# Writing and reading back the third attention's turned weights in two halves

## The reference, cut to what matters

```python
q = (xq @ Wq + bq).reshape(B, L, 16, 16)              # 4 x 1024 rows, 16 heads of 16
k, v = ...                                            # 77 keys, from the context
scores = einsum('bqhd,bkhd->bhqk', q, k) / sqrt(16)
attn = softmax(scores, axis=-1)                       # the weights: 16 x 77 per row
out = einsum('bhqk,bkhd->bqhd', attn, v).reshape(B, L, 256)
return x_q + (out @ Wp + bp)
```

## Time and profile before

| | us |
|---|---|
| median of 3 runs (lowest, highest) | 991.32 (990.92, 993.13) |
| the profiled execution's own time | 993.48 |
| its span, from the first to the last instruction | 991.7 |
| TensorE busy | 931.4 (94%) |
| VectorE busy | 869.5 (88%) |
| ScalarE, GpSimd busy | 743.9 (75%), 701.0 (71%) |
| DMA packets of 16 engines | 205354 |

### The profile page before, as it was taken

How to read it: one execution, slowest core, us unless ns; L and a number is a source line. 1 busy time by engine, 2 the same in 40 slices (tenths; PEclk the granted TensorE clock), 3 DMA queues, 4 the chain that set the end, 5 groups by cost and what they waited for, 6 DMA issues and landing times. The chain is left out here.

```text
span 991.7 us, 32386 instructions
## 1 busy us (share of the span) xinstructions
PE 931.4 (94%) x10500; PEld 812.2 (82%) x10500; DVE 869.5 (88%) x4318; ACT 743.9 (75%) x1604; POOL 701.0 (71%) x1099
## 2 busy tenths in 40 slices
PE   6987899999999999999999999999999999998996
PEld 3775788888889898888888888888888888787884
DVE  2469999999999999999999999999999999887643
ACT  2345788888878888888878787888887887787763
POOL 1227867877777788787777777788777777666752
PEclk9679999999999999999999999999999999999999
DMA  8277200033333332223333332222333332210000
GB/s 285 61 145 136 65 18 18 15 75 74 72 71 76 77 75 51 61 56 75 76 69 72 76 76 51 63 62 67 76 72 70 76 77 52 60 37 7 6 7 18
DMA packets 205354, 66.43 MB, mean 67 GB/s; under 512 B 186520, under 2 KB 198961, under 8 KB 204546
## 3 DMA queue, kind: packets, MB, share of 16 engines
q1 hardware_dynamic: 205186, 64.35, 29.4%
HBM read 39.02 MB, written 25.30 MB: 65 GB/s over the span
## 5 line engine op out<-in xcount | busy, mean ns | idle before, releaser
L2333 PE MATMUL ps<-hT_C,w_m_sb 128*128 128x128 f32 x2048 | 256.6, 278 | 1.8 <-DVE hidden_C L1663 1.5
L2333 PEld LDWEIGHTS ps<-hT_C,w_m_sb 128*128 128x128 f32 x2048 | 243.6, 192 | 14.4 <-issue 8.2
L1032 ACT ACTIVATE silu_C<-ps,cols_sb 128x128 f32<-128x128 f32 x256 | 93.5, 366 | 120.0 <-PE ps L2333 115.5
L2344 PE MATMUL ps<-w_m_sb,hidden_C 128*128 128x256 f32 x512 | 121.1, 380 | 0.2
L1569 DVE MATCH_REPLACE8 scores_left_B<-mx_B,scores_left_B 128x77 f32<-128x77 f32 x512 | 108.4, 225 | 0.0
L1565 DVE MATCH_REPLACE8 scores_left_B<-mx_B,scores_B 128x77 f32<-128x77 f32 x512 | 108.1, 223 | 0.0
L2344 PEld LDWEIGHTS ps<-w_m_sb,hidden_C 128*128 128x128 f32 x512 | 92.7, 190 | 10.9 <-DVE hidden_C L1663 0.7
L650 POOL TENSOR_TENSOR p_B<-scores_B,mx_B 128x616 f32<-128x616 f32 x64 | 78.4, 1226 | 26.3 <-DVE mx_B L1563 24.9
L655 POOL TENSOR_TENSOR scores_D<-scores_D,mx_D 128x616 f32<-128x616 f32 x62 | 76.0, 1225 | 25.1 <-DVE mx_D L1636 25.1
L1663 DVE SCALAR_TENSOR_TENSOR hidden_C<-ps,cols_sb,silu_C 128x128 f32<-128x128 f32 x256 | 83.7, 337 | 9.7 <-ACT silu_C L1032 9.5
L1517 DVE TENSOR_REDUCE mx_A<-ps 128x8 f32<-128x1024 f32 x64 | 75.3, 1219 | 11.8 <-PE ps L2235 11.2
(11 more groups left out here) (188 smaller groups left out, 2451.7 us busy)
## 6 DMA issues: line engine op xcount, KB each, us to landing
p_turned_D<-p_blocks_D SPq DMA_DIRECT2D x100, 160.0 KB, 3.9
pT_D<-p_turned_D SPq DMA_DIRECT2D x25, 640.0 KB, 4.0
xn_turned_A<-xn_blocks_A SPq DMA_DIRECT2D x124, 32.0 KB, 2.0
xn_A<-xn_turned_A SPq DMA_DIRECT2D x31, 128.0 KB, 2.1
x_A<-in_x SPq DMA_DIRECT2D x28, 128.0 KB, 3.3
out<-y_D SPq DMA_DIRECT2D x28, 128.0 KB, 2.5
w_m_sb<-in_w_m SPq DMA_DIRECT2D x3, 1024.0 KB, 5.2
w_mod_sb<-in_w_mod SPq DMA_DIRECT2D x2, 1024.0 KB, 9.5
```

What stands on the lines that cost most here:

```text
L1032: sc.activation(SA[:, j, :], bank(f"C.up{j}")[:, 0:P], ACT.Silu, bias=col("bm1_a", j)).then_inc(sa_ok, 1)
L2333: ins = mm(bank(f"C.up{j}")[:, half * P:(half + 1) * P], w_m1[:, k, m:m + P], HT["C"][:, t % HT_COPIES["C"], k, :], start=(k == 0), stop=( ...
L2344: ins = mm(bank("C.dn0")[:, 0:CH], G[:, t % G_COPIES, j, :], w_m2[:, j, :], start=(j == 0), stop=(j == HJ - 1))
```

## The change

The DRAM tensor gets the half as its first dimension. `write_weights` and `read_weights` are called once per half: the write of a half waits for that half's turned blocks alone, and there are eight DMAs of half the size for four, and two reads for one. Each half has its own semaphores. `weigh_values` waits for half 0 before its first eight matmuls and for half 1 before the other eight. From the second such tile on, a write also waits for the read of the tile before. One load (`w_qd`) shares a semaphore with `w_q`, for which the first queries of B and D now both wait.

```diff
-        weights_turned = {s: nc.dram_tensor(f"p_turned_{s}", [ROWS, QUAD, NCH, ROWS, QUAD], F32, kind="Internal").ap()
+        weights_turned = {s: nc.dram_tensor(f"p_turned_{s}", [KC, ROWS, QUAD, HCH, ROWS, QUAD], F32, kind="Internal").ap()
...
-            def write_weights(t, s):
+            def write_weights(t, s, c):
                 if not weights_by_transfer(t, s):
                     return
-                sp.wait_ge(pb_ok[s], KC * (weight_transfers(t, s) + 1))
+                n = weight_transfers(t, s)
+                sp.wait_ge(pb_ok[s], KC * n + c + 1)
+                if n > 0:
+                    sp.wait_ge(pt_in[s][c], 16 * n)
                 for i in range(ROWS):
-                    sp.dma_start(weights_turned[s][:, :, :, i, :].rearrange("j k n q -> k n j q"),
-                                 PB[s][quad(i), :].rearrange("k (n j q) -> k n j q", n=NCH, j=ROWS)).then_inc(pb_out[s], 16)
-
-            def read_weights(t, s):
+                    sp.dma_start(weights_turned[s][c, :, :, :, i, :].rearrange("j k n q -> k n j q"),
+                                 PB[s][quad(i), c * HALF_COLS:(c + 1) * HALF_COLS].rearrange("k (n j q) -> k n j q", n=HCH, j=ROWS)
+                                 ).then_inc(pb_out[s][c], 16)
+
+            def read_weights(t, s, c):
...
-                sp.wait_ge(pb_out[s], 16 * ROWS * (weight_transfers(t, s) + 1))
+                sp.wait_ge(pb_out[s][c], 16 * ROWS * (weight_transfers(t, s) + 1))
                 sp.wait_ge(pv_ps[s], t)
-                sp.dma_start(PT[s][:].rearrange("p n q -> p (n q)"),
-                             weights_turned[s].rearrange("j k n i q -> (j k) (n i q)")).then_inc(pt_in[s], 16)
+                sp.dma_start(PT[s][:, c * HCH:(c + 1) * HCH, :].rearrange("p n q -> p (n q)"),
+                             weights_turned[s][c].rearrange("j k n i q -> (j k) (n i q)")).then_inc(pt_in[s][c], 16)
...
-                run(write_weights, i, 8, "D")
+                run(write_weights, i, 8, "D", 0)
+                run(write_weights, i, 8, "D", 1)
                 run(load_next_x, i, 0)
                 run(store_y, i, 9)
-                run(read_weights, i, 8, "D")
+                run(read_weights, i, 8, "D", 0)
+                run(read_weights, i, 8, "D", 1)
...
-            load_weights(w_qd[:], a["Wq"], "d")
+            load_weights(w_qd[:], a["Wq"], "b")
...
-                    dve.wait_ge(pb_out[s], 16 * ROWS * n)
+                    dve.wait_ge(pb_out[s][c], 16 * ROWS * n)
...
-                    pe.wait_ge(ld[{"A": "qkv", "B": "b", "D": "d"}[s]], 16)
+                    pe.wait_ge(ld["qkv" if s == "A" else "b"], 16 if s == "A" else 16 * 2)
...
             def weigh_values(t, s):
-                if weights_by_transfer(t, s):
-                    pe.wait_ge(pt_in[s], 16 * (weight_transfers(t, s) + 1))
-                else:
+                if not weights_by_transfer(t, s):
                     pe.wait_ge(pt_ok[s], 3 * weights_transposed(t, s) + 3)
...
                 for c in range(KC):
+                    if weights_by_transfer(t, s):
+                        pe.wait_ge(pt_in[s][c], 16 * (weight_transfers(t, s) + 1))
```

More of the change, by code:

```diff
@@ L214, in block_kernel @@
         ld = {n: sem(f"ld_{n}") for n in ("cond", "small", "mod_a", "mod", "gate", "rows", "qkv", "so",
-                                          "b", "kv_b", "kv_d", "up", "down", "d", "ctx")}
+                                          "b", "kv_b", "kv_d", "up", "down", "ctx")}
         silu_done, zeroed, masks_ok, rows_ok = (sem(n) for n in (
@@ L250, in block_kernel @@
         xb_ok, xb_out, xt_in = ({s: sem(f"{n}_{s}") for s in TURNED} for n in ("xb_ok", "xb_out", "xt_in"))
-        pb_ok, pb_out, pt_in = ({s: sem(f"{n}_{s}") for s in WEIGHTS_TURNED} for n in ("pb_ok", "pb_out", "pt_in"))
+        pb_ok = {s: sem(f"pb_ok_{s}") for s in WEIGHTS_TURNED}
+        pb_out, pt_in = ({s: numbered(f"{n}_{s}", KC) for s in WEIGHTS_TURNED} for n in ("pb_out", "pt_in"))
         tmp_ok, yd_ok, y_out = sem("tmp_ok"), sem("yd_ok"), sem("y_out")
@@ L487, in drain @@
                 store_y(TILES - 9)
-                write_weights(TILES - 8, "D")
-                read_weights(TILES - 8, "D")
+                write_weights(TILES - 8, "D", 0)
+                write_weights(TILES - 8, "D", 1)
+                read_weights(TILES - 8, "D", 0)
+                read_weights(TILES - 8, "D", 1)
                 write_turned(TILES - 1, "A")
@@ L492, in drain @@
                 store_y(TILES - 8)
-                write_weights(TILES - 7, "D")
-                read_weights(TILES - 7, "D")
+                write_weights(TILES - 7, "D", 0)
+                write_weights(TILES - 7, "D", 1)
+                read_weights(TILES - 7, "D", 0)
+                read_weights(TILES - 7, "D", 1)
                 store_y(TILES - 7)
```

## The result

The changed kernel takes 980.88 us (median; 980.28 to 984.83), the kernel before 992.23 (990.92 to 993.17; these are the three executions known before and one more). The ratio is 0.9897, 95% interval 0.9872 to 0.9922: 10.2 us, with 7.7 to 12.7 inside the interval. The forecast was 984.6 us, with a range from 982.5 to 989.5. The way came as forecast, and so did the wait that goes; the size was half as large again. Two executions further down, one of E2 (2691 us) and one of E4 (1840 us), were disturbed, and the medians and ratios leave them out.

What follows compares the result with a forecast made beforehand. VectorE was taken to bound every round, losing only TensorE's lateness beyond some 0.4 us. Listed waits of 6.6 us plus 0.3 made 6.9 us gone, taking 991.3 to 984.4, stated as 984.6 us, range 982.5 to 989.5.

Steps and rivals of the forecast that it cites:

- the wait that goes: VectorE's wait for `scores_a` ahead of `mx_A` would fall from 6.6 us to under 1; likeliest rival, chance 0.72.
- The chain: Late read of turned weights delays TensorE's `weigh_values`, which delays VectorE's `mx_A` by whatever exceeds some 0.4 us.
- The earlier start: Writes of half 0 start on SP after the first half's turn, 1.3 us before the second turn ends.
- the issues: Eight half-size writes on SP at 0.63 us each take 5.0 us, ending 3.7 us after the second turn.
- the queue of SP: After writes, x and y, SP is free and issues read 0 5.7 us after the second turn, read 1 at 6.0.
- The rule of the Trainium skill: Spoke against the change: small DMAs cost about 2 us fixed, and two transfers to disjoint halves serialize.
- The fit weighed there: DMA time as 2.0 us plus bytes at 436 GB/s: two serial reads of 320 KB would take 5.5 us.
- the sum: VectorE's 6.6 us of listed waits plus 0.3 us gives 6.9 us gone, median from 991.3 to 984.4.
- small gaps that would stay: Some 2.7 us of the 8.7 lost over 22 rounds, in scattered gaps on VectorE the change doesn't touch.
- The wait in the middle: TensorE's wait for half 1 inside `weigh_values`: cost bounded from nothing to 3.9 us, taken as nothing.
- my slack of 1.3 us for half 1: Half 1 would land 9.7 us after the second turn, 1.3 us before `weigh_values` needs it.

Runs made afterwards that it cites:

- E2: The changed kernel, unchanged, run again in more rounds: 980.90 us, ratio 0.9884 against the kernel before.
- E4: The kernel before with its four whole writes, but two reads by halves and two waits of TensorE: 986.91 us, ratio 0.9934.
- E1: The kernel before, unchanged, against itself: 990.88 us, ratio 0.9985.
- E12: The kernel before, unchanged, profiled a third time: one run, 995.98 us.
- E3: The changed kernel with its early half-size writes, but one read for both halves and one wait of TensorE: 985.49 us, ratio 0.9917.
- E11: Same kernel as E4 (the kernel before with two reads and two waits), run again for an undisturbed profile: 985.34 us, ratio 0.9934.
- E5: The changed kernel, but both halves' writes wait for both turns, so no earlier start: 998.64 us, ratio 1.0055 against the kernel before.
- E8: The changed kernel with the four writes of half 1 cut into eight, twelve writes in all: 1034.54 us, ratio 1.0415 against the kernel before.
- E7: The changed kernel with the load of `w_qd` on its own semaphore again: 981.57 us, ratio 0.9893 against the kernel before.
- E6: The changed kernel, but TensorE waits for both halves before its first matmul of `weigh_values`: 984.40 us, ratio 0.9912 against the kernel before.
- E10: The kernel before with its one read ahead of the load of x and the store of y: 991.24 us, ratio 1.0013.
- E9: The changed kernel with both reads ahead of the load of x and the store of y: 981.09 us, ratio 0.9903 against the kernel before.

## Why the prediction was off

*The chain* was right but for half of its last link. VectorE loses what TensorE is late beyond 0.4 us, and TensorE is late by the read. But the read is late in two ways, and I saw one: it is issued late because the writes land late (T0 + 7.7 in the round of the earlier trace rows), or it is issued in time and lands late itself. One of the worst rounds of before is of the second kind (timeline of all engines, 748 to 765 us; T0 is 749.24):

```profile
748.41 0.83 DVE L1509 STREAM_TRANSPOSE p_blocks_D<-p_D 128x640 f32<-128x640 f32 x1
...
756.16 0.32 SPq L410 DMA_DIRECT2D pT_D<-p_turned_D  x1
...
761.44 1.08 PE L2311 MATMUL ps<-pT_D,vblk_D 128*32 128x128 f32 x32 [1.67 <-DMA pT_D<-p_turned_D]
```

The read goes at T0 + 6.9, which by the prediction costs next to nothing, and TensorE starts 5.3 us behind it, not 4.0. Rounds whose read goes before T0 + 7.0 hold 4.0 of the 8.4 us of lateness in this profile, 7.4 of 11.7 in E1 and 5.8 of 10.0 in E12: more than half in all. That fits E3, where an earlier read alone doesn't cure it, and E11, where waiting part by part helps though the reads go as late as before. With the wait gone `mx_A` starts 13.05 to 13.11 us after T0 in 22 of 23 rounds, and at 13.42 in the other.

*The earlier start, the issues, the queue of SP* came nearly as worked out: T0 - 1.28 for - 1.3, 0.65 us an issue for 0.63, the eight done at T0 + 4.1 for 3.7, read 0 at T0 + 5.4 to 6.6, 6.1 at the median, for 5.7. The rule of the Trainium skill weighed there ("DMA: Bandwidth & Descriptors", "Rules for kernel authors") says that two transfers to disjoint partition halves serialize and aren't worth it. It did not decide here, where each half is half the columns of all 128 partitions: E11 gains some 6 us by two reads for one alone. E5 and E8 show where more and smaller transfers lose, in the time to issue: without the lead eight issues are a loss, and four more than the changed kernel's eight cost over 50 us (1034.5 against 981). The fit weighed there is, in the Trainium skill ("DMA: Bandwidth & Descriptors", "Anatomy of one DMA"), one of DMAs that GpSimd issues; by it a read of 320 KB would take 2.8 us, an estimate. SP issues the reads here, and in the changed kernel one of 320 KB landed 3.5 us after its issue at the median, which decides.

*The step that failed is the sum*: "What counts is VectorE's part: 6.6 us listed, plus [...] 0.3 us. 6.9 us are gone." That term was too small twice over.

- The list of waits under-reads. In the same profile the lateness by T0 is 8.4 us. The list leaves out small waits and shows the others some 0.1 short. The spacing of the rounds had said 8.7 plus the 0.8 of the first round; I put 2.7 of it down to small gaps that would stay (by the rows it is 2.9: 8.7 less the 6.6 listed, of which 0.77 belong to the first round and not to the spacing). Some 1.1 us stayed: the changed kernel has three rounds of 27.60 us, in places where before has long rounds too.
- One execution isn't the kernel. Three profiles of before have 8.4, 11.7 and 10.0 us, mean 10.0; three with the changed path (first profile, E2, E7) 0.4, 1.5 and 0.6, mean 0.8. The difference is 9.2 us, against 10.2, 11.5 and 10.6 by the ratios of the three. The profile I worked from has the lowest lateness of the three of before. But all three are of executions above the median (993.5, 996.4 and 996.0 us against 990.8 to 993.3 in the sets), so their mean may be on the high side.

*The wait in the middle* had the wrong sign. I looked for what it costs (0 to 3.9 us). E6 shows that it brings some 2 to 3: a read lands 4.0 us behind its issue at the median but up to 5.8 (before; a half 3.5 and up to 5.4, changed), and my slack of 1.3 us for half 1 was worked out from the median. What two parts and two waits give is room for late landings.

*How the parts share the gain,* by one profile each. Lead alone: lateness 3.9 (E3). Two reads alone: 4.8 (E11). Both with one wait: 4.4 (E6). All three: 0.8. From 10.0, each part takes most of the loss by itself and they overlap; halves without the lead make it 13.3, since they are paid in issues on SP.

*Open.* The ratios lie 1.0 to 2.3 us above the difference in lateness. All three profiles of before and E10 start late (first `mx_A` at 28.8 to 28.9 us), while of nine profiles with split reads or writes seven start at 26.2 to 27.0. The start counts in full: each of the thirteen profiled executions' own time, less its lateness and its first `mx_A`, is 953.6 to 957.2 us. The six that start late are all 1.2 us or more above the median of their kernel, up to 5.5; of the seven others six are within 1.6 of theirs (E6 is 2.2 above). From 12 to 30 us the granted clock is 0.85 or 0.86 in the six and 0.88 to 1.00 in the seven. That fits a start that is drawn anew in each execution and goes with the clock there; but no experiment touched the start, and whether the change makes the late one rarer isn't known. Nor is it known what makes single landings late. In the round of E8 shown above `mx_A` stands 3.62 us after TensorE's start, where 2.22 and the 0.86 of the stretched step make 3.08; the other 0.5 us wasn't looked into.

## What to carry to other kernels

Measure a loss by the distance between two events of a round that is fixed when nothing is late, over all rounds, and in more than one profile: a list of waits shows less, and a DMA's lateness differs from one execution to the next. Where a transfer lies on the path, plan for the worst landing, not the median; splitting it and waiting part by part buys room for it even where the bytes are the same. Every further DMA costs its issue on the queue that everything else stands in, so split only where something pays for that: two reads for one won 0.7% by themselves, eight writes for four on top made it 1% with a lead of 1.3 us, and without the lead a loss of 0.5%.

## What I had not expected of the hardware

An issue of a DMA with a four-dimensional pattern takes 0.57 us at best and 0.61 to 0.65 at the median, whether it moves 32 or 80 KB, or 40 and 80 mixed (E8); at 160 KB it is 0.57 and 0.90. Leaving x and y out from behind the writes (E10) doesn't let the writes land sooner. The kernel before scattered from 986.65 to 999.42 us over 23 runs on one chip, the changed path from 978.45 to 983.51 over 6 beside it (E9). The landings that vary may be the cause of the wider spread. No run isolates it, and six executions scatter less than 23 by their number alone.
